# Second-layer attention regrouped to four maps of 32 columns, with denominators summed by VectorE and GpSimd; ternary steps redistributed

## The reference

```
q, k: 16 maps (8 heads x 2), 16 channels each; v: 8 heads, 32 channels
p_m  = softmax(mask(q_m k_m^T * scale))           causal, 1024 x 1024 per map
y_h  = (p_h1 @ v_h) - lam * (p_h2 @ v_h)
out  = (1 - 0.2) * (y @ wo^T)
```

```
scale = clip(mean(|w_g|), 1e-8);  q = clip(round(w_g / scale), -1, 1)
w_used = w + ((q * scale) - w)                    in bf16
```

## Time and profile before

| | us |
|---|---|
| median of 3 runs | 4462.45 (4454.85 to 4469.24) |
| profiled execution, own time | 4468.33 |
| its span in the profile | 4466.6 |
| PE busy | 3635.4 (81%) |
| DVE busy | 2574.3 (58%) |
| ACT busy | 1904.4 (43%) |
| POOL busy | 850.4 (19%) |

### The profile page before, as it was taken

One profiled execution on the slowest core, in us unless ns is written; L12 is line 12 of the kernel. 1 busy time (PEld: TensorE's weight loads), 2 busy tenths in 40 slices (PEclk: granted clock), 3 DMA queues, 4 the chain that ended last, 5 costly groups with the idle time before them and its releaser, 6 DMA issues. The chain is left out here.

```text
span 4466.6 us, 62749 instructions
## 1 busy us (share of the span) xinstructions
PE 3635.4 (81%) x23244; PEld 2181.8 (49%) x23244; DVE 2574.3 (58%) x5320; ACT 1904.4 (43%) x2923; POOL 850.4 (19%) x1022
## 2 busy tenths in 40 slices
PE   5776786768768888888893888987988888898897
PEld 3424333235166373554732666655653653663672
DVE  5756665647465454554546455455665665764764
ACT  2262461542656566464662434343126126216206
POOL 3012111120122030110302223232311220220220
PEclk8987897888889999898995989998999999999999
DMA  5411403214140000000002000002000000000000
GB/s 187 123 40 62 128 29 120 75 62 123 34 152 1 5 25 6 24 1 29 1 6 78 1 29 29 5 24 78 1 1 29 1 1 29 1 1 29 1 1 10
DMA packets 147087, 177.10 MB, mean 40 GB/s; under 512 B 16384, under 2 KB 123392, under 8 KB 146688
## 3 DMA queue, kind: packets, MB, share of 16 engines
q1 hardware_dynamic: 139008, 153.81, 10.9%
q0 software_dynamic: 6144, 16.79, 1.1%
q10 hardware_dynamic: 1632, 2.49, 0.2%
HBM read 126.40 MB, written 51.38 MB: 40 GB/s over the span
## 5 line engine op out<-in xcount | busy, mean ns | idle before, releaser
L708 DVE TENSOR_REDUCE arena<-ps 128x2 f32<-128x1024 f32 (+3 forms) x768 | 698.8, 953 | 170.6 <-PE ps L676 96.4
L906 ACT ACTIVATE arena<-ps 128x1024 f32<-128x1024 f32 (+3 forms) x768 | 576.6, 811 | 162.9 <-PE ps L813 111.8
L989 DVE TENSOR_TENSOR arena<-arena,tri 128x256 f32<-128x256 f32 x512 | 210.2, 423 | 354.5 <-ACT arena L906 325.2
L813 PE MATMUL ps<-arena 64*128 64x512 f16 (+3 forms) x1536 | 261.7, 355 | 163.3 <-ACT arena L906 99.0
L830 PE MATMUL ps<-arena 128*17 128x512 f32 (+3 forms) x3072 | 350.8, 531 | 6.4 <-DVE arena L989 4.1
L906 ACT ACTIVATE attention<-ps 128x1024 f32<-128x1024 f32 (+3 forms) x384 | 287.5, 810 | 142.7 <-PE ps L813 142.6
L2557 ACT ACTIVATE arena<-ps 128x256 f32<-128x256 f32 x192 | 63.6, 381 | 620.2 <-PE ps L2499 574.9
L813 PEld LDWEIGHTS ps<-arena 64*128 64x128 f16 x1536 | 71.1, 94 | 521.8 <-ACT arena L906 404.4
L830 PE MATMUL ps<-attention,live 128*33 128x512 f32 (+3 forms) x1536 | 290.8, 502 | 0.0
L676 PE MATMUL ps<-arena 64*128 64x512 f16 (+3 forms) x1536 | 238.2, 336 | 54.0 <-DVE arena L708 47.3
L1158 PE MATMUL ps<-gated_parts,weight_parts 128*128 128x256 f32 x1536 | 216.2, 298 | 30.4 <-DVE operands L1258 30.4
(11 more groups left out here) (324 smaller groups left out, 7094.6 us busy)
## 6 DMA issues: line engine op xcount, KB each, us to landing
arena<-w_experts SPq DMA_DIRECT2D x128, 256.0 KB
acc<-sums SPq DMA_DIRECT2D x16, 1024.0 KB, 5.9
x_next<-sums SPq DMA_DIRECT2D x16, 1024.0 KB, 8.5
arena<-slots_x SPq DMA_DIRECT2D x32, 512.0 KB, 4.6
slots_y<-arena SPq DMA_DIRECT2D x32, 512.0 KB, 4.3
sums<-acc SPq DMA_DIRECT2D x24, 512.0 KB, 2.9
making<-basis SPq DMA_DIRECT2D x16, 768.0 KB, 6.5
slots_x<-arena SPq DMA_DIRECT2D x1, 4096.0 KB, 29.5
```

Of the source, the lines that this page charges most:

```text
L708: dve.reduce_max(a.mp[:, 2 * j:2 * j + 2, qt, c], out[:, :, 0:w], AX.X).then_inc(self.pair_out, 1)
L813: last = pe.matmul(m.ps[:, 4 + 2 * (v % 2) + odd, q0:CH], a.k[half, pair, kt * P:(kt + 1) * P], a.q[half, pair, c * CH + q0:(c + 1) * CH], ...
L906: act.activation(a.p[:, v % ring, :, q0:CH], m.ps[:, b:b + 2, q0:CH], ACT.Exp, scale=HD ** -0.5).then_inc(exped, 1)
L989: dve.tensor_tensor(diag, diag, keep, ALU.min).then_inc(masked, 1)
```

## The change

1. The second layer's attention is called with `4, 32` and a new flag `apart=True`: 4 groups of 4 maps, each with all 32 columns of the value. There is no column left for the ones, so the denominators are summed apart.
2. A step with `kt = 0` writes its exponentials to a buffer of totals (6 places) instead of the ring. The exponentials of later key tiles are added to it in place, elementwise, both maps at once. `added_by` tells the engine: DVE for key tiles 1 to 3 of chunk 1 (`add_total`, L1080 of the changed kernel), POOL for all tiles on the diagonal but `kt = 0` (L836). A place of the ring is free for a new exponential only when the value product and the addition have both read it.
3. When a group is complete, PE multiplies the four totals by a column of ones placed at the group's column (`sum_total`), DVE adds the result into one tile (`keep_total`), and at the end of a chunk PE turns this tile (`turn_totals`) and DVE inverts it (`invert`). `give` then has three instructions on 256 columns for a query tile, instead of ten on 4, 8 or 128 columns.
4. Every attention stage, those of the first and fourth layer too, has 7 more semaphores.
5. In `ternary_weights` the scale is spread to full width by ACT, DVE does the product with it and the last two steps for all three parts, and POOL does nothing.

```diff
+    def added_by(n):
+        c, g, kt = units[n]
+        if kt == 0:
+            return None
+        return "vector" if c == 1 and kt < TC else "pool"
...
+    in_ring = [v for v in range(pairs * n_units) if not apart or units[v // pairs][2] > 0]
+    ring_place = {v: i for i, v in enumerate(in_ring)}
+    totalling = {last_of[unit] + lag + 2: unit for unit in range(NC * groups)} if apart else {}
+    sums_turning = groups * TC + lag + 3
...
+                    for j in range(pairs):
+                        pool.wait_ge(masked, pairs * diagonals[n] + j + 1)
+                        if kt == 1:
+                            pool.wait_ge(summed, n)
+                        elif added_by(n - 1) == "vector":
+                            pool.wait_ge(vector_added, additions("vector", n - 1) + j + 1)
+                        else:
+                            pool.wait_ge(pool_added, additions("pool", n - 1) + j + 1)
+                        t = total(c * groups + g, j)[:, :, q0:CH]
+                        pool.tensor_tensor(t, t, probabilities(pairs * n + j)[:, :, q0:CH],
+                                           ALU.add).then_inc(pool_added, 1)
...
+            def sum_total(unit):
+                n, g = last_of[unit], unit % groups
...
+                pe.wait_ge(evac, unit + 1)
+                pe.wait_ge(pool_added, additions("pool", n + 1))
+                for hh in range(maps):
+                    last = pe.matmul(m.ps[width * hh:width * hh + width, unit % 2, :],
+                                     a.column[:, g * width:(g + 1) * width], total(unit, hh // 2)[:, hh % 2, :],
+                                     start=True, stop=True)
+                last.then_inc(totalled, 1)
...
-                if v >= ring:
-                    act.wait_ge(summed, (v - ring) // pairs + 1)
+                if apart and units[n][2] == 0:
+                    held = (pairs * (units[n][0] * groups + units[n][1]) + v % pairs - a.total.shape[1]) // pairs
+                    if held >= 0:
+                        act.wait_ge(totalled, held + 1)
+                elif ring_place[v] >= ring:
+                    old = in_ring[ring_place[v] - ring]
+                    act.wait_ge(summed, old // pairs + 1)
+                    if apart and added_by(old // pairs) == "vector":
+                        act.wait_ge(vector_added, additions("vector", old // pairs) + old % pairs + 1)
+                    elif apart:
+                        act.wait_ge(pool_added, additions("pool", old // pairs) + old % pairs + 1)
...
+            def add_total(n):
+                c, g, kt = units[n]
+                for j in range(pairs):
+                    dve.wait_ge(exped, pairs * n + j + 1)
...
+                    t = total(c * groups + g, j)
+                    dve.tensor_tensor(t, t, probabilities(pairs * n + j), ALU.add).then_inc(vector_added, 1)
...
-                        attention_scratch(a, Arena(words), NM // 2, 6)
-                        attention(nc, m, a, 2, 64, wo, 1.0 - LAMBDA_INIT, b, store=into[2])
+                        attention_scratch(a, Arena(words), NM // 4, 6, 6)
+                        attention(nc, m, a, 4, 2 * HD, wo, 1.0 - LAMBDA_INIT, b, store=into[2], apart=True)
...
-                dve.tensor_tensor(g3(q1), g3(q1), bc(f.sc[:, :]), ALU.mult).then_inc(scaled, 1)
...
+                dve.wait_ge(scale_spread, i + 1)
+                step(dve.tensor_tensor(q1, q1, f.spread[:, :], ALU.mult))
+                step(dve.tensor_tensor(q1, q1, wb, ALU.subtract))
+                dve.tensor_tensor(q1, q1, wb, ALU.add).then_inc(ready, 1)
```

More of the change, by code:

```diff
@@ L734, in sync_rows, with attention @@
         self.sync_end(sp)
-def attention(nc, m, a, maps, width, wout, out_scale, batch, store=None, routed=None):
+def attention(nc, m, a, maps, width, wout, out_scale, batch, store=None, routed=None, apart=False):
     groups, pairs = NM // maps, maps // 2
@@ L756, in attention @@
               [("turn", half) for half in range(halves)] + ([("back", 0), ("project", 0)] if wout is not None else [])]
-    finishing = {groups * TC // per_block + lag + 1 + i: place for i, place in enumerate(spaced)}
+    finishing = {groups * TC // per_block + lag + (5 if apart else 1) + i: place for i, place in enumerate(spaced)}
     in_a_row = [(step, k - d) for k in range(TC + 2) for step, d in (("project", 2), ("turn", 0), ("back", 1))
@@ L776, in attention, with total, probabilities @@
+    sums_turning = groups * TC + lag + 3
+    def total(unit, j):
+        return a.total[:, (pairs * unit + j) % a.total.shape[1]]
+    def probabilities(v):
+        n, j = divmod(v, pairs)
+        c, g, kt = units[n]
+        if apart and kt == 0:
+            return total(c * groups + g, j)
+        return a.p[:, ring_place[v] % ring]
     with stage(nc, "scored", "exped", "masked", "summed", "evac", "turned", "steps", "given", "y_turned", "y_stored",
-               "projected", "added", *(NextNormalisation.SEMAPHORES if store is not None else ()),
@@ L824, in values @@
                 if kt == 0 and unit >= 2:
-                    pe.wait_ge(evac, unit - 1)
+                    pe.wait_ge(totals_kept if apart else evac, unit - 1)
                 for hh in range(maps):
@@ L841, in turn @@
                         pe.wait_ge(ahead.kept, NT // 2)
+                if apart and u == 0:
+                    pe.wait_ge(inverted, 1)
                 if c == 0 and u >= 1:
@@ L887, in _ @@
                     ahead.tensor_turn(pe, block - NEXT_TURN, 2 + (block - NEXT_TURN) % 2)
+                if block in totalling:
+                    sum_total(totalling[block])
+                if apart and block == sums_turning:
+                    turn_totals(0)
                 if block in finishing:
@@ L890, in _ @@
             pe.wait_ge(exped, n_units * pairs)
+            if apart:
+                sum_total(NC * groups - 1)
+                turn_totals(1)
             for piece, j in in_a_row:
@@ L934, in give @@
                 heads = CH // width
-                r = m.small[:, half * heads:(half + 1) * heads]
+                r = m.small[:, 0:heads]
                 y = a.y[:, t % 2, half * D // halves:(half + 1) * D // halves]
                 dve.wait_ge(turned, u + 1)
-                if maps == 4:
+                if not apart:
                     y3 = y.rearrange("p (h c) -> p h c", c=HD)
@@ new lines, in keep_total @@
+            def keep_total(unit):
+                dve.wait_ge(totalled, unit + 1)
+                if unit >= 1:
+                    dve.wait_ge(totals_kept, unit)
+                if unit % groups == 0:
+                    if unit:
+                        dve.wait_ge(totals_turned, unit // groups)
+                    dve.tensor_copy(a.totals[:, :], m.ps[:, unit % 2, :]).then_inc(totals_kept, 1)
+                else:
+                    dve.tensor_tensor(a.totals[:, :], a.totals[:, :], m.ps[:, unit % 2, :],
+                                      ALU.add).then_inc(totals_kept, 1)
@@ L1017, in attention_live, with attention_scratch @@
     return a
-def attention_scratch(a, ar, groups, ring):
+def attention_scratch(a, ar, groups, ring, totals):
     a.o = ar.take(groups + groups // 4 + 1, CH)
@@ L1023, in attention_scratch @@
     a.yt = ar.take(2, D)
-    a.z = ar.take(2, D // 2)
+    a.z = ar.take(D)
     a.p = ar.take(ring, 2, CH)
+    a.total = ar.take(totals, 2, CH)
+    a.totals = ar.take(CH)
+    a.column = ar.take(CH // 4)
 def attention_memory(m, ar, heads, vd, groups, ring):
@@ L2817, in program @@
                 f.raw = ar.take(3, part)
+                f.spread = ar.take(part, dtype=BF16)
                 f.wb = ar.take(3, part, dtype=BF16)
```

114 lines of the change are left out of this document (80 added, 34 removed).

## The result

The changed kernel takes 4625.85 us (median of 4 runs, 4616.21 to 4638.45) where the kernel before takes 4459.85 us beside it (4 runs). The ratio is 1.037, with a 95% interval of 1.035 to 1.039. It is slower, by 166 us.

A forecast was written before the change was run, and what follows sets the result against it. PE bounds the attention before; after, a queue shared by POOL's additions, DVE's additions and masks, with holes. 4468.3 + 156 - 9 + 5 = 4620, 4614 for a median, 4 lower for holes filled: 4610 us, range 4530 to 4670.

The forecast's parts named there:

- They exclude each other: Second-layer attention: POOL's additions, DVE's additions and masks form one queue, 23.0 us a group in chunk 1, 11.0 in chunk 0.
- Chunk 0: First part of a second-layer attention stage: POOL starts after 6.2 us, then the queue is full, 51 us in all.
- The chain in chunk 1: Second-layer attention: waits leave holes of 4 us in the queue, 27 us a group, 105.5 us for the chunk.
- the ring of three tiles: Chunk 1: tile 3's exponential needs tile 7's place from the group before, a cause of the queue's holes.
- The tail: End of a second-layer attention stage: 19.5 us instead of 25.3, counted as -6; 21.5 at half clock.
- Stage: One second-layer attention stage: 42 + 3 - 6 = +39 us, times 4: +156 us.
- Ternary weights: The ternary weights stage, once: a faster scale product and no waits for POOL, -8.9 us in sum.
- Semaphores: Seven more names in each of 12 stages at 0.4 us: +5 us, bounds 0 and 7.
- A: Rival: the queue is always full, without holes, 143 us until the last addition, +21 a stage, 4548 us; chance 0.2.
- B: Rival: no exclusion, each engine at its own speed, +1 us a stage, 4468 us, no change; chance 0.07.
- C: Rival: additions hide wholly and ACT bounds as in the fourth layer, -29 us a stage, 4348 us; chance 0.07.
- D: Rival: clock at half level in chunk 1, +1.8 us a group, +7 a stage, tail 21.5, 4646 us; chance 0.2.

The follow-up runs named there:

- e7: Changed kernel with each POOL addition replaced by three fills of the same places, so POOL writes but reads nothing: stage 158.5 to 159.3 us, ratio 1.016.
- e13: Changed kernel with ring of 8, 4 totals, product of totals two blocks later in chunk 1, DVE's additions before masks: stage 174.5 to 177.6 us, ratio 1.031.
- e10: Changed kernel with a ring of 8 places instead of 6 and 4 totals instead of 6: stage 183.2 to 188.2 us, ratio 1.037.
- e8: Changed kernel with DVE's additions put ahead of the block's masks in its program: stage 174.1, then 178.1 to 178.4 us, ratio 1.032.
- e12: Changed kernel with ring of 8, 4 totals, and PE's product of totals two blocks later in chunk 1: stage 180.7 to 181.7 us, ratio 1.035.
- e1: Kernel before with the new ternary weights alone, attention and semaphores as before: 4337.05 us against 4349.23, ratio 0.997.
- e3: Changed kernel without any of the additions, all else kept: stage 119.5 to 120.1 us, ratio 0.979.
- e5: Changed kernel with POOL's additions alone, DVE's left out: stage 163.8 to 164.4 us, ratio 1.019.

## Why the prediction was right, point by point

The forecast was 4610 us, slower. 4625.85 is inside the range and 16 us above it. The change was forecast at +148 us over the median and measured at +166. What costs the time was named rightly, but several sizes were off and partly cancelled.

**What bounds, and the prices.** PE bound the attention, and PE would stop being the bound: right, as PE was busy 75 of 116 us of chunk 1. POOL's 1024-column additions take 2.34 us (the first of a group, 3.20, waits 0.86 of them for DVE), which is the 2.35 of the fit from the earlier trace rows. DVE's took 1.22, as in the earlier trace rows.

**They exclude each other.** Right, and shown by e7, where POOL only writes and the masks are 0.42 us again. But the prediction counted every mask as 0.42 us of the queue, and that is too much: the last group of e13 is full and takes 20.9 us where its sum is 23.0. Its own rows held a sign of this. The DVE addition of the earlier trace rows ended 0.29 us after POOL's, not the 0.43 that it needs alone, so not all of it stood behind POOL. One of its signs was wrong too. The prediction expected DVE's additions "lengthened to 2 or 3 where POOL is at work". In the changed kernel no addition of DVE is lengthened, because none starts inside POOL's work. The masks carry it, 64 of them with 0.68 us each on top. By the rule of the Trainium skill ("SBUF — State Buffer", Who interferes with whom) a GpSimd instruction that only writes does not contend with a two-input DVE instruction. The trace of e7 agrees: 0.42 us beside fills, 1.10 beside additions.

**Chunk 0.** 51 us forecast, 48.4 measured, and this is near for partly wrong reasons. The six additions of a group take 8.2 to 8.4 us where the queue has 11.0 with its masks, but in front of the three later groups POOL waits 1.7, 1.3 and 5.1 us for PE's value products, for which the prediction had nothing.

**The chain in chunk 1.** 105.5 us and 3 for the pieces were forecast, 115.8 measured. This is the term that was mis-sized, and two errors in it partly cancel, which is luck. The prediction let the queue be full from the start of tile 4 on, "and inside it the two additions of the next group's tile 1", 16.4 us a group behind a chain of 10.5. In the trace POOL's part is 13.55 to 13.75 us, as the masks hardly lengthen it and no addition of DVE is inside it. In four groups this is 8.6 us less than forecast. The holes are 17.9, 16.3, 15.1 and 11.9 us, together 61.1 where 42 and 3 for the pieces were forecast, 16 more. The additions of tile 1 stand behind `keep_sums` in DVE's order, and so come only at 1850.44 in the hole shown, 4.7 us behind POOL's last addition. That moves the whole chain. The pieces bring the waits for PE shown there (2.06 and 2.28 us), where I priced them at 0.4 us of DVE each. Even without pieces the last hole is 11.9 us. Together it is 7 us a stage.

**What is behind the holes.** The prediction named the ring of three tiles and masks ahead of additions. e10 shows that the ring is not it. e8 gives 9 us a stage to the order of masks and additions, and e12 some 5 to PE's place for the product of totals. Why e13 doesn't have the sum of both isn't settled.

**The tail.** 19.5 us forecast, 22.9 to 23.2 measured in three batches and about 19 in the third. The granted clock is 0.50, the low level, in the former and 0.76 in the latter. I took a value between the two levels, and the low one was the case. This costs 3.4 us a stage. For the low level itself the prediction had 21.5, which is 1.4 us too short. The tail of before, which it took as one at the low level, has a granted clock of 0.62 over its 25.3 us.

**Stage.** -2.6 us in chunk 0, +7.3 in chunk 1, +3.4 in the tail: +8 on the forecast +39 gives the measured +47 (+42 in the batch whose tail ran at the higher clock).

**Ternary weights.** -8.9 forecast, -9.1 measured, and e1 shows that it comes through to the end. **Semaphores.** +5 forecast, some +4 measured. From the end of the last DVE instruction of an attention stage to the start of the next stage it is 2.19, 2.19 and 2.59 us behind the first three of the second layer in the kernel before, and 2.51 behind each of them in the changed one. Over the eleven attention stages that another one follows it is 34.4 us before and 33.9 in e1, and 37.7 to 38.2 in the eleven kernels with exactly the seven more.

**The rivals.** A (no holes, 143 us until the last addition) falls: 164 were measured. B (no exclusion, no change) falls twice. There is an exclusion, and e7, in which it is lifted, is still 19 us a stage slower than before. C (additions hidden) would at best have been e3 without any addition, 0.979 of the time before. D was partly true. The clock fell to 0.50 in the tail, and the tail's 3.4 us are its part. In chunk 1 it fell to its low level too, but where POOL adds and PE waits for masks. In the holes, where D put its cost, the granted clock is 0.79 to 0.95 and the eight half products mostly last 1.06 or 1.07 us, as the row of the product of totals in the third hole does too (1.06), so the 1.8 us a group of D are not seen there. What slower products cost at the borders of the stretches isn't shown.

**Where the 47 us lie.** The new form without additions gains 20 us (e3). POOL's additions cost 44 (e5), DVE's on top 23. Without the exclusion both together cost 39 instead of 67 (e7).

## What to carry to other kernels

An addition of two SBUF operands on GpSimd is not free help for VectorE when VectorE has such operations too. In this kernel it held VectorE's masks up until its end, and it took twice as long a column (2.11 against 1.04 ns): the same additions on VectorE alone were 26 us a stage faster. Before moving work to GpSimd, list what VectorE does in the meantime and how many of its operations read two SBUF operands. And follow the program order of an engine that feeds another one: here VectorE's additions stood behind a copy and pieces that waited for PE, and those waits were in the chain, not only the durations.

## What the runs showed of the hardware that was not expected

A GpSimd fill of 1024 fp32 columns (0.96 us) leaves VectorE's two-operand instructions alone, while an addition holds them for up to its whole length: a mask of 0.42 us took 2.57. The price is not the same both ways. Six such masks lengthened eight GpSimd additions (12.3 us by their own prices) only to some 13.1 in the last group of e13, while two VectorE additions of 1024 columns lengthened them by 2.4 us in e10.

TensorE's granted clock stood at 0.50 while GpSimd added in chunk 1 and TensorE was busy 3.7 to 8.2 of 13.7 us, and rose to 0.79 to 0.95 in the holes between. It stayed at 0.50 through a whole tail in three batches (16.7 of 23.5 us busy), where the tail of the third batch was granted 0.76 (12.0 of 19.5 us busy). What made the difference isn't seen in these rows.
